# Three whole transfers that form h + x + b_out in step 3, against 75 small ones spread over steps 1 and 2

## The reference, cut to what matters

```
h    = silu(LN(x) @ W_in.T + b_in)
# six steps of diffusion over the graph
out = term = h
for i in 1..6:  term = (mean of term over the incoming edges) / i;  out += term
x    = x + out @ W_out.T + b_out
x    = x + experts(LN(x))          # 8 experts, top 2
```

## Time and profile before

| | |
|---|---|
| median of 3 runs | 1383.98 us (1383.05 to 1384.16) |
| the profiled execution, its own time | 1385.32 us |
| its span, first to last instruction | 1383.5 us |
| TensorE busy | 1192.7 us, 86% of the span |
| VectorE busy | 728.0 us, 53% |
| ScalarE busy | 368.1 us, 27% |
| GpSimd busy | 158.1 us, 11% |
| granted TensorE clock, mean | 0.929 |

### The profile page before, as it was taken

The page is one execution under the profiler, slowest core; times in us unless marked ns, Lnnn a source line. Parts: engine busy times, 40 slices in busy tenths (PEclk is TensorE's granted clock), DMA queues, the critical chain, the costliest instruction groups (busy, mean ns, idle before and its releaser), DMA issues.

```text
span 1383.5 us, 27811 instructions
## 1 busy us (share of the span) xinstructions
PE 1192.7 (86%) x7796; PEld 826.7 (60%) x7796; DVE 728.0 (53%) x1480; ACT 368.1 (27%) x722; POOL 158.1 (11%) x171
## 2 busy tenths in 40 slices
PE   4895999999999999999369999988999359999870
PEld 2784776665666666666146666655666338777750
DVE  7588999963443343431135344324554755555545
ACT  1574655540000000010012111101211224344333
POOL 2000000000000000000000000000111224565540
PEclk8897999999999999999679999999999559999995
DMA  6110010023211112147753233211433111222229
GB/s 156 31 53 19 24 39 30 30 56 97 62 49 59 53 53 69 41 153 142 81 127 110 69 97 103 72 29 57 122 112 106 49 31 56 77 68 70 71 62 255
DMA packets 74762, 105.04 MB, mean 76 GB/s; under 512 B 11939, under 2 KB 60891, under 8 KB 74491
## 3 DMA queue, kind: packets, MB, share of 16 engines
q1 hardware_dynamic: 62500, 72.44, 18.2%
q0 software_dynamic: 9824, 24.61, 7.7%
q10 hardware_dynamic: 2356, 6.93, 2.0%
HBM read 76.99 MB, written 37.49 MB: 83 GB/s over the span
## 4 chain that ended last, share of the span: by engine, by line
PE 66%; DMA 10%; issue 9%; DVE 8%; ACT 2%; POOL 2%; DVEq 1%; another core or an unknown queue 1%; SPq 1%; ACTq 1%; POOLq 0%
PE ps L1647 35%; PE ps L1625 7%; PE ps L1777 5%; PE ps L1693 4%; PE ps L1761 4%; PE ps L1593 4%; DMA w_dram<-v_a 3%; DVE v_b L1059 3%; DMA v_a<-L_ffn_W 2%; DMA adj<-y_dram 2%; PE ps L1561 2%; PE ps L1572 1%; DMA v_b<-xs_dram,v_a 1%; DMA h_ring<-h_dram 1%
## 5 line engine op out<-in xcount | busy, mean ns | idle before, releaser
L1647 PE MATMUL ps<-v_b,adj 125*125 125x512 f16 x1250 | 275.7, 384 | 37.0 <-DVE t_hi L1066 35.0
L1647 PE MATMUL ps<-v_a,adj 125*125 125x512 f16 x1375 | 297.3, 379 | 0.0
L1647 PEld LDWEIGHTS ps<-v_b,adj 125*125 x1250 | 172.8, 138 | 139.7 <-issue 43.0
L1647 PEld LDWEIGHTS ps<-v_a,adj 125*125 (+1 forms) x1375 | 187.6, 137 | 108.9
L1059 DVE TENSOR_TENSOR v_b<-v_b 125x2560 f16<-125x2560 f16 x125 | 180.2, 1485 | 7.1 <-PE ps L1593 6.5
L1066 DVE SCALAR_TENSOR_TENSOR t_hi<-ps,cinv,t_hi 125x256 f32<-125x256 f32 x125 | 60.2, 482 | 222.2 <-ACT t_hi L820 222.2
L820 ACT ACTIVATE t_hi<-ps,cinv 125x256 f32<-125x256 f32 x125 | 59.0, 472 | 421.9 <-PE ps L1647 383.6
L1693 PE MATMUL ps<-v_b,adj 125*125 125x512 f16 x625 | 143.4, 389 | 5.1 <-DVEq L1234 3.3
L797 ACT ACTIVATE adj<-ps 125x625 f32 (+1 forms) x125 | 111.8, 906 | 75.2 <-PE ps L1593 74.4
L1625 PE MATMUL ps<-v_a,adj 125*125 125x512 f16 x500 | 123.4, 380 | 0.0
L1761 PE MATMUL ps<-v_b,adj 128*128 128x128 f16 x1344 | 116.9, 222 | 6.5 <-issue 5.1
(11 more groups left out here) (235 smaller groups left out, 914.9 us busy)
## 6 DMA issues: line engine op xcount, KB each, us to landing
h_ring<-h_dram SPq DMA_DIRECT2D x125, 125.0 KB
v_a<-L_ffn_W SPq DMA_DIRECT2D x32, 256.0 KB, 3.5
v_b<-L_ffn_W SPq DMA_DIRECT2D x32, 256.0 KB, 3.2
adj<-w_dram SPq DMA_DIRECT2D x16, 512.0 KB, 4.8
w_dram<-w_hi SPq DMA_DIRECT2D x32, 128.0 KB, 1.9
hx_dram<-h_dram POOLq DMA_DIRECT2D x1, 3125.0 KB, 13.0
hx_dram<-x POOLq DMA_DIRECT2D x1, 3125.0 KB, 20.3
hx_dram<-L_gnn_b_out POOLq DMA_DIRECT2D x1, 3125.0 KB, 63.6
```

What stands on the lines that cost most here:

```text
L1647: last = te.matmul(ps[0:NP, u, :], of_tile(adj[0:NP, 0:ADJ], i, u, a * NP, NP), source[:, a, :], start=(a == 0), stop=(a == T - 1))
```

## The change

The three transfers are cut by rows into HX = 25 parts of 125 rows. Part n is a copy, an add of x and an add of b_out, each followed by a wait for its landing, and goes out when `tile_ps` has reached 26 + 2n: with the first tile of step 1 and then with every second tile, the last one with the 24th tile of step 2. The parts stand in POOL's list ahead of the wait for `w_top_ok` and the reduction. In the branch that isn't taken the parts are issued once more after `h_dram` has been rewritten. SP waits for 48 x 25 in place of 48.

```diff
+    HX = 25
+    HX_EVERY = 2
...
-            sp.wait_ge(S["hx_ok"], 48)
+            sp.wait_ge(S["hx_ok"], 48 * HX)
...
+            def sums(n, done):
+
+                part = slice(n * N // HX, (n + 1) * N // HX)
+                rows = N // HX
+                g.dma_start(hx_dram[part, :], h_dram[part, :]).then_inc(S["hx_ok"], 16)
+                pool.wait_ge(S["hx_ok"], done + 16)
+                g.dma_start(hx_dram[part, :], x[part, :], max_dma_last_dim=8192, accum_op=ALU.add).then_inc(S["hx_ok"], 16)
+                pool.wait_ge(S["hx_ok"], done + 32)
+                g.dma_start(hx_dram[part, :], bass.AP(b_out.tensor, 0, [[0, rows], [1, D]]), accum_op=ALU.add).then_inc(S["hx_ok"], 16)
+                pool.wait_ge(S["hx_ok"], done + 48)
+
+            for slot in range(3):
+                pool.wait_ge(h_out[slot], H_OUT[slot])
+            for n in range(HX):
+                pool.wait_ge(S["tile_ps"], T + 1 + n * HX_EVERY)
+                sums(n, 48 * n)
 
             pool.wait_ge(S["w_top_ok"], 1)
             g.partition_all_reduce(w_all, w_top, 128, bass.bass_isa.ReduceOp.max).then_inc(S["w_all_ok"], 1)
...
-
-            for slot in range(3):
-                pool.wait_ge(h_out[slot], H_OUT[slot])
-            g.dma_start(hx_dram, h_dram).then_inc(S["hx_ok"], 16)
-            pool.wait_ge(S["hx_ok"], 16)
-            g.dma_start(hx_dram, x, max_dma_last_dim=8192, accum_op=ALU.add).then_inc(S["hx_ok"], 16)
-            pool.wait_ge(S["hx_ok"], 32)
-            g.dma_start(hx_dram, bass.AP(b_out.tensor, 0, [[0, N], [1, D]]), accum_op=ALU.add).then_inc(S["hx_ok"], 16)
+                for n in range(HX):
+                    sums(n, 48 * (HX + n))
+                pool.wait_ge(S["hx_ok"], 96 * HX)
```

More of the change, by code:

```diff
@@ L54, in gnn_ffn @@
     LAG = 3
+    HX = 25
+    HX_EVERY = 2
+    assert N % HX == 0 and T + 1 + HX * HX_EVERY <= 3 * T + 1
     assert FT % FU == 0
```

## The result

The changed kernel took 1347.84 us (median of 4 executions, 1345.46 to 1350.90) against 1384.07 us: ratio 0.974, 95% interval 0.9718 to 0.9762, that is 33 to 39 us less. The profiled execution took 1345.46 us (span 1343.6), 39.9 us less than that of before. The forecast was 1344 us, with a range of 1341 to 1355.

The account below looks back on a forecast made before the run. TensorE was taken to bound the kernel, stalled in step 3 by POOL's three whole transfers. Profiled 1385.32 us less 40.3 gives 1345.0, the median 1343.7; with 0.3 us for small things 1344, range 1341 to 1355.

Parts of the forecast that it names:

- TensorE loses 40.3 us in step 3: Step 3: two stalls and slow matmuls cost TensorE 40.3 us, all hanging on hx_dram traffic, all regained by the change.
- The chain of a part, c = 9.8 us: POOL, steps 1 and 2: a part's three chained transfers take 9.8 us, under the 10.8 us spacing, so no lag.
- The surcharge for adding x: In each part on POOL: adding x costs a 25th of (20.3 - 13.0) us more, 0.3 us.
- A late reduction is free up to 20.4 us: Head of step 3: TensorE's five banks cover a reduction up to 20.4 us late; 1.6 us expected, cost zero.
- The prediction's own sign of being wrong: Head of step 3: the reduction well after 606 us and VectorE waiting at L1158 would show the forecast wrong.
- No contention in steps 1 and 2: Steps 1 and 2: the parts' traffic costs other transfers 0 to 5 us at two boundaries, taken as 0.
- POOL's constants at the last step: POOL before L691: the 7.29 us issue gap stays, costing zero, or up to a few us if it grows.
- The sum: Whole kernel: profiled 1385.32 us less 40.3 gives 1345.0; the median 1343.7, with 0.3 us for small things 1344.
- The rivals on the spacing: POOL's parts outlast their spacing and delay the reduction: slower above 13.1 us a part, chance 0.07; nearly fitting, 0.05.
- they fit nearly: POOL, steps 1 and 2: a part takes 11.5 to 13.1 us, loss 0 to 40 us; chance 0.05.
- The rule to coalesce: POOL's transfers: by the skill's fit 75 small ones take 172 us, three whole 28; a part's sum stays unchanged.
- The engines of the b_out transfer: The b_out add on POOL: 5 engines for 3125 rows and for 125, so the same rate whole or cut.

Follow-up runs that it names:

- after_again: The changed kernel run again with no edit: 1346.01 us against 1384.14 for the kernel before, ratio 0.9723.
- start_late: The changed kernel with all 25 releases of parts four tiles later: 1364.37 us, ratio 0.9852 to the kernel before.
- reduce_first: The changed kernel with the wait for w_top_ok and the reduction ahead of the last two parts: 1346.88 us, ratio 0.9729 to the kernel before.
- waves: The changed kernel with each part's three transfers overlapped with its neighbours' in 27 waves: 1347.59 us, ratio 0.9729 to the kernel before.
- waves_step3: The kernel before with its three whole transfers replaced, in their place in step 3, by 27 overlapped waves of small ones, without releases: 1348.64 us, ratio 0.9743.
- no_b_out: The kernel before with the add of b_out left out, the copy of h and add of x still whole: 1347.16 us, ratio 0.9724.
- whole_early: The kernel before with its three whole transfers moved to step 1, released when tile 26 ends: 1367.98 us against 1384.45, ratio 0.9873.

## Why the prediction was right, step by step

- *TensorE loses 40.3 us in step 3, all under `hx_dram` traffic, and gets it back.* Right: 40.5 us, in the trace after. Leaving out b_out alone gives it back too, so it was one of the three transfers. The prediction had counted all three as one. It set its weight load of 27.58 us beside the 1.9 us of a store; loads of that size land in 3.5 us otherwise, which changes nothing.
- *The chain of a part, c = 9.8 us.* Mis-sized: 11.44 us, and 11.27 in the other two traces with that list (`after_again`, `start_late`). From the starts of the 75 issues the mean from copy to add of x is 3.10 us (2.5 forecast), from there to the add of b_out 3.75 (2.8), from there to the next copy 4.56 (4.5). The term for b_out, a 25th of its whole, came out near: 1.8 us over a plain copy for 2.0. Two were not right. The surcharge for adding x was taken as a 25th of (20.3 - 13.0), 0.3 us; copying x in place of adding it shows 1.0 us. So most of it comes with each transfer and not with its bytes. And the median of a copy, 2.4 us, is near the 2.2 forecast, but 5 of the 25 copies took 4.0 to 4.9 us from their start to the next issue. What delays these wasn't tried and stays open.
- *A late reduction is free up to 20.4 us.* Right, and that saved the forecast: 18.3 us cost nothing, 34.8 us cost a break of 14.98. The prediction's own sign of being wrong did come, the reduction well after 606 us and VectorE waiting for it (L1158, now L1173). It had no lag in its sum and got one of 18.3 us. That c stopped at 11.44, just short of the 11.5 where the lag starts to cost, was luck; that there was room up to there was worked out.
- *No contention in steps 1 and 2.* Right: 1.1 us of waiting for `h_ring`.
- *POOL's constants at the last step.* Right: the gap before the `iota` was 7.15 us, before 7.29, and the second tile of the last step began 9.17 us after the first, before 9.30. The 0.6 us between 40.5 and 39.9 are 0.3 us ahead of step 1 and 0.3 us behind step 4.
- *The sum.* 1385.32 - 39.9 = 1345.4 was measured where 1345.0 was forecast. The two medians, 1347.84 and 1346.01, lie 2 to 4 us above 1344, and so do those of the other four kernels in which TensorE has no break in steps 1 to 4 and the last step isn't held up (`reduce_first`, `waves`, `waves_step3`, `no_b_out`: 1346.88 to 1348.64). By their medians all six gain 36 to 38 us, not 40.3. That needs neither the late reduction nor the small parts, since `no_b_out` has neither. In the two traced executions over 1347 us (`no_b_out`, `waves_step3`) steps 1 to 4 take 539.80 us, and from there to the last instruction it is 474.5 and 475.0 us, before 472.7 and in the change 473.0. So some 2 us of it lie behind step 4; what makes them stays open.
- *The rivals on the spacing* had the right mechanism, a lag that builds up, and "they fit nearly" came close: c = 11.44 against 11.5, where it starts to cost.
- *The rule to coalesce* of the Trainium skill (DMA: Bandwidth & Descriptors, rules for kernel authors) held in its cost and not in its advice here: the 75 transfers took 2.4, 3.3 and 4.1 us, some 245 us in sum for 96.9 us of the three whole ones, and the kernel is 36 us faster, as nothing has to wait for them and the short ones let others through.
- *The engines of the b_out transfer.* By the Trainium skill (DMA: Bandwidth & Descriptors, why a DMA increments its semaphore by 16 and not by 1) b_out would be on 5 engines whole or cut. The landing times (63.6 us, and 4.1 a part) agree with an unchanged rate, and no run here counts the engines. The prediction read a DMA share of 0.45 in 645 to 650 us as "not spread over sixteen", which doesn't follow: from 660 to 665 us, in the same transfer, the share was 0.87, and in `whole_early` it was 0.97 over the 64 us from 370 to 434 us, in which b_out ran.

## What to carry to other kernels

A transfer that nobody waits for can still bound the kernel: read what its neighbours on the queues waited for while it ran, and whether one of a chain (here a row repeated 3125 times) outlasts what the waiting engines can cover. Before moving chained transfers, set their cycle time against their spacing, count what is queued behind them on the issuing engine (here the reduction in one place and the constants of the last step in the other), and don't price a small add as its share of a large one. How much lateness the banks behind an engine can take is a number to work out first: here 20.4 us, and the change used 18.3 of it.

## What the runs showed of the hardware that I hadn't expected

- Adding one row of 1 KB to 3125 rows takes 63.6 us, in some 3152 packets; adding 3125 different rows, whole, takes 20.9, in 416. Beside the first, a row block of 125 KB on SP's queue takes up to 22.72 us (step 1), and in step 3 it kept VectorE waiting for 28.16 us; beside the second a row block took 14.62 us; beside small pieces of the same work VectorE waited 1.1 us in 55 tiles.
- With the add a transfer of 125 KB takes about 1.0 us (x) and 0.6 us (b_out, whose packets differ too) more than without.
- POOL stands 7.1 to 7.3 us in "issue" before its first `iota` of the last step, before, in the change, and with the transfers overlapped or back in step 3.
